# The place of one load of x among the set-up transfers of SyncE's queue in a fused two-block transformer kernel

## What is computed

```
m = silu(cond) @ w_ada + b_ada                     # nine rows: shift, scale, gate x 3
x = x + gate * self_attn(ln(x) * (1+scale) + shift)       # A: windows of 128 rows, 16 heads
x = x + gate * topk_cross_attn(ln(x) * (1+scale) + shift, ctx)   # B: best 16 of 77 keys
x = x + gate * swiglu(ln(x) * (1+scale) + shift)          # C: 256 -> 2 x 1024 -> 256
kv = modulated layernorm(ctx)                       # the second context
x = x + cross_attn(modulated layernorm(x), kv) @ Wp + bp  # D: softmax over 77 keys
```

## Time and profile before

| | |
|---|---|
| median of 3 runs | 1042.06 us (1039.88 to 1044.54) |
| the profiled execution's own time | 1043.68 us |
| its span, first to last instruction | 1041.9 us |
| mean granted TensorE clock | 0.971 of full |
| TensorE busy (matmul) | 983.6 us, 94% |
| VectorE, ScalarE, GpSimd busy | 834.8, 782.9, 705.4 us |
| load of x, two per tile | 64 transfers in all, median 2.2 us to landing |
| store of y, two per tile | 64 transfers in all, median 2.1 us |

### The profile page before, as it was taken

The page is one execution under the profiler, slowest core; times in us unless marked ns, Lnnn a source line. Parts: engine busy times, 40 slices in busy tenths (PEclk is TensorE's granted clock), DMA queues, the critical chain, the costliest instruction groups (busy, mean ns, idle before and its releaser), DMA issues.

```text
span 1041.9 us, 33051 instructions
## 1 busy us (share of the span) xinstructions
PE 983.6 (94%) x10980; PEld 868.1 (83%) x10980; DVE 834.8 (80%) x4234; ACT 782.9 (75%) x1681; POOL 705.4 (68%) x1100
## 2 busy tenths in 40 slices
PE   6885699999999999999999999999999999999985
PEld 5563588898888898889988888988999888888874
DVE  2356789989888888889898888888898988888631
ACT  1143478888888888888888888888888888888662
POOL 2257355777777778777777777787777777767754
PEclk9788699999999999999999999999999999999996
DMA  8305000000000000000000000000000000000000
GB/s 294 42 27 125 32 7 8 7 12 13 13 13 11 4 12 12 13 13 12 12 12 12 13 10 4 13 12 12 13 13 12 12 12 8 7 8 7 7 6 16
DMA packets 33848, 23.14 MB, mean 22 GB/s; under 512 B 22979, under 2 KB 31427, under 8 KB 33168
## 3 DMA queue, kind: packets, MB, share of 16 engines
q1 hardware_dynamic: 33680, 21.02, 7.8%
HBM read 16.19 MB, written 4.83 MB: 20 GB/s over the span
## 4 chain that ended last, share of the span: by engine, by line
PE 87%; issue 3%; DMA 3%; DVE 3%; SPq 2%; ACT 2%; POOL 2%; POOLq 0%; DVEq 0%; ACTq 0%
PE ps L1242 21%; PE ps L1251 10%; PE ps L1123 9%; PE ps L1231 8%; PE ps L1220 7%; PE ps L1204 7%; PE ps L1195 4%; PE ps L1154 3%; PE ps L1171 3%; PE ps L1184 3%; PE ps L1112 2%; PE ps L1134 2%; PE ps L1144 2%; DMA w_mod_sb<-in_w_mod 1%; PE ps L1053 1%
## 5 line engine op out<-in xcount | busy, mean ns | idle before, releaser
L1242 PE MATMUL ps<-hT_C,w_m_sb 128*128 128x128 f32 x2048 | 250.7, 275 | 0.2 <-DVE hidden_C L934 0.2
L1242 PEld LDWEIGHTS ps<-hT_C,w_m_sb 128*128 128x128 f32 x2048 | 241.6, 192 | 2.7 <-issue 0.7
L678 ACT ACTIVATE silu_C<-ps,cols_sb 128x128 f32<-128x128 f32 x256 | 90.7, 367 | 72.9 <-PE ps L1242 72.0
L503 POOL TENSOR_TENSOR p_D<-scores_D,rc_D 128x616 f32<-128x616 f32 x64 | 78.2, 1225 | 79.1 <-DVE rc_D L905 79.1
L503 POOL TENSOR_TENSOR p_B<-p_B,rc_B 128x616 f32<-128x616 f32 x64 | 77.8, 1217 | 67.4 <-DVE p_B L891 66.1
L1251 PE MATMUL ps<-w_m_sb,hidden_C 128*128 128x256 f32 x512 | 121.0, 379 | 0.0
L934 DVE SCALAR_TENSOR_TENSOR hidden_C<-ps,cols_sb,silu_C 128x128 f32<-128x128 f32 x256 | 87.9, 344 | 33.4 <-ACT silu_C L678 33.0
L883 DVE MATCH_REPLACE8 scores_left_B<-mx_B,scores_left_B 128x77 f32<-128x77 f32 x512 | 108.3, 223 | 0.0
L879 DVE MATCH_REPLACE8 scores_left_B<-mx_B,scores_B 128x77 f32<-128x77 f32 x512 | 108.1, 222 | 0.2 <-issue 0.2
L1251 PEld LDWEIGHTS ps<-w_m_sb,hidden_C 128*128 128x128 f32 x512 | 94.6, 190 | 11.4
L833 DVE TENSOR_REDUCE mx_A<-ps 128x8 f32<-128x1024 f32 x64 | 75.4, 1221 | 26.8 <-PE ps L1154 26.6
(11 more groups left out here) (180 smaller groups left out, 2574.6 us busy)
## 6 DMA issues: line engine op xcount, KB each, us to landing
x_A<-in_x SPq DMA_DIRECT2D x64, 64.0 KB, 2.2
out<-y_D SPq DMA_DIRECT2D x64, 64.0 KB, 2.1
w_mod_sb<-in_w_mod SPq DMA_DIRECT2D x2, 1024.0 KB, 11.9
w_m_sb<-in_w_m SPq DMA_DIRECT2D x1, 2048.0 KB, 7.6
w_m_sb<-in_w_m SPq DMA_DIRECT2D x1, 1024.0 KB, 10.0
w_qkv_sb<-in_w_qkv SPq DMA_DIRECT2D x1, 768.0 KB, 5.8
w_gate_sb<-in_w_gate SPq DMA_DIRECT2D x1, 768.0 KB, 7.5
rows_sb<-in_rows SPq DMA_DIRECT2D x1, 768.0 KB, 8.8
```

Of the source, the lines that this page charges most:

```text
L503: g.tensor_tensor(where, src, rc, ALU.mult).then_inc(n_ok[s], 1)
L678: sc.activation(SA[:, j, :], bank(f"C.up{j}")[:, 0:P], ACT.Silu, bias=col("bm1_a", j)).then_inc(sa_ok, 1)
L1242: ins = mm(bank(f"C.up{j}")[:, half * P:(half + 1) * P], w_m1[:, k, m:m + P], HT["C"][:, t % HT_COPIES["C"], k, :], start=(k == 0), stop=( ...
```

## The change

In SyncE's `body` the loading of the MLP weights moves from the head of body 4 to its end, and the rearrangement of the second context ("D") moves from the end of body 3 to the end of body 4, ahead of the MLP weights. So the load of x for tile 4 (the fifth), which stands in body 4, is now issued before both, and the two keep their order between themselves.

```diff
             def body(i):
-                if starts(i, 4):
-                    load_mlp_weights()
                 run(load_next_x, i, 0)
                 run(store_y, i, 9)
                 if starts(i, 2):
                     set_up_flat("B")
                     load_context_weights()
-                if starts(i, 3):
+                if starts(i, 4):
                     set_up_flat("D")
+                    load_mlp_weights()
```

## The result

The changed kernel takes 1032.91 us (median of 5 runs, 1028.8 to 1034.12) against 1042.06 (median of 5); the ratio is 0.9909, with a 95% interval of 0.9891 to 0.9928. Repeated in two further sessions it gave 0.9921 (0.9899 to 0.9943) and 0.9931 (0.9911 to 0.9952). So it is 0.7 to 0.9% faster, 7.2 to 9.4 us by the medians, clear of the 0.5% that can be told from nothing. Its profiled execution has a span of 1032.3 us and a time of 1034.12; the span before was 1041.9.

What follows compares the result with a forecast made beforehand. TensorE bounds the long middle; before it, VectorE stalls 10.94 us for x behind 3 MB in the same queue. A gain of 8.9 - 0.4 = 8.5 us on the median of 1042.06 gives 1033.5 us, range 1029 to 1038.

Steps and rivals of the forecast that it cites:

- (a): SyncE's load of x for tile 4: issued at about 66.4 us, so VectorE's stall of 10.94 us goes wholly.
- (b): SyncE's rearrangement and MLP weights, now behind the load's wait: start as before, cost nothing, at most 1 us.
- (c): TensorE after VectorE's statistics of tile 4: restarts at 97.97 us, 10.9 us earlier.
- (d): ScalarE's copies wait for GpSimd's clearing until 103.1 us; 2.0 of 10.9 us are spent there, L1184 moves by 8.9.
- (e): From L1184 on everything moves by 8.9 us, carried to the end; VectorE waits about 4 us before ev_A.
- (f): GpSimd's vblk_D beside a working VectorE: stays at 4.95 us, with an upper bound of about 6.9.
- rival of a slow vblk_D: GpSimd's vblk_D becomes slow beside VectorE: gain 6.9 us, 1035.2 us; chance 0.08.
- (g): TensorE's clock at L1184 after idle time: half clock costs nothing or about 0.9 us; 0.4 taken.
- a rival with a chance of 0.15: TensorE's half-clock stretch at 125 to 131 us need not recur: gain 11 to 13.5 us, 1028.6 to 1031; chance 0.15.
- rival of the instructions caught in the flood of transfers: Engines' instruction fetches held up by full DMA engines at 98 to 107 us: gain 1.7 to 6 us; chance 0.08.

Runs made afterwards that it cites:

- held: The changed kernel, with the fifth load of x also waiting for the normalisation of tile 3: 1043.32 us, ratio 1.0021 to the kernel before.
- no_pad_wait: The changed kernel without ScalarE's wait for GpSimd's clearing: 1030.90 us, ratio 0.9891 to the kernel before; in another session (_b) 1030.50 us.
- mlp_first: The changed kernel with the MLP weights issued ahead of the rearrangement, behind x: 1034.22 us, ratio 0.9924 to the kernel before.
- x_between: The kernel before, with the fifth load of x issued between the two MLP weights: 1038.73 us against 1041.65, ratio 0.998.
- x_behind_flat: The kernel before, with the fifth load of x ahead of the MLP weights but still behind the rearrangement: 1032.24 us, ratio 0.9907.

## Why the prediction was right

The forecast was 1033.5 us, a gain of 8.5; measured are 1032.91 and 9.2 in the first session. By its steps:

- (a) held: xn_A was the last to come, x was issued at 65.40 (66.4 said), and st_A stands without a wait at 96.05 (96.3).
- (b) held, and the run *held* gives its price: once the wait ends after the values are ready, each us costs one.
- (c) held: TensorE restarts at 97.74 (97.97).
- (d) was the step that mattered, and held: the clearing ends at 103.52 (103.06), the copies start at 103.60, and no_pad_wait shows that it is this wait. It is 0.5 us later than I had it, since the whole rearrangement is 0.7 later in this execution. What it costs was mis-sized: I had 2.0 us. Removing it brought 2.9 and 3.7. With L1204 at half clock, as I had reckoned, L1184 starts 19.6 us after the start of the rearrangement (no_pad_wait) instead of 22.0 (the changed kernel's first trace), 2.4 us earlier, and its 32 matmuls run at full clock, 1.08 us instead of 2.15 (106.90 to 109.05): the wait costs by the clock too, and I had kept the two apart. With L1204 at full clock L1184 starts 17.3 us after it (no_pad_wait_b), but then GpSimd's queue is the limit: o_A is 3.1 us earlier than in the changed kernel of that session.
- (e) held in its second half: the TensorE-bound middle carries the shift to the end, as the last column shows. Its first half, that from L1184 on everything moves alike, did not: the first matmul of the MLP moved 9.85 us where ev_A moved 7.4 (see g). And VectorE waits 5.69 us before ev_A, not about 4, for ev_A comes 1.5 us later than I had it.
- (f) held: vblk_D takes 4.95 us beside a working VectorE, to the digit the value of before, and its instructions 1271 to 1275 ns each. The rival of a slow vblk_D fell. The two slow ones of vblk_B lie beside w_out_B again. With the rule that I had set beside it (the Trainium skill, SBUF — State Buffer, "Who interferes with whom") the trace agrees for w_out_B (2261 ns for the slowest of vblk_B beside it). MATCH_REPLACE and MAX8 ran beside all of vblk_D and cost it nothing. I had MATCH_REPLACE read two tiles; in the timeline it is two instructions, MATCH_VALUE_LOAD and MATCH_REPLACE8, so it is no test of a rule on two inputs of one instruction. The price of that rival, 6.9 us, left the 0.4 us of (g) out; by my own sum it would have been 6.5, and 1035.5.
- (g) is the term that was mis-sized, in both its halves. L1219 and L1183 both ran at half clock, so that the 32 matmuls of L1183 took 2.15 us instead of 1.08: 1.1 us, where I had taken 0.4 of a possible 0.9. They also started 0.4 us later than I had them (106.90, for 106.5), from the later clearing of (d). So ev_A moved by 7.4 us, not 8.9 or 8.5. Against that, the low stretch behind ev_A was missing: 2.5 us, which I had put into a rival with a chance of 0.15. That the sum came out this close was luck: these errors cancelled. The other traces of the changed kernel have the low stretch partly (1.61 us for L1153) and nearly wholly (2.04), and the two further sessions gave 9.4 and 7.2 us.

The rival of the instructions caught in the flood of transfers fell with the changed kernel itself: TensorE restarts at 97.74 us and L1183 at 106.90, and the DMA share of that kernel's window 97 to 107 us is 0.93. Without the wait for the clearing all engines run through the flood, at a DMA share of 0.84 (columns as in the earlier trace rows):

```profile
96.00:107.00 11.00, 7.76 (x115) 6.32 (x115) 9.34 (x67) 6.09 (x11) 10.38 (x15) 0.84 0.84 305
```

It also fell with mlp_first, where the flood lies at 66 to 78 us beside four engines that work (TensorE is busy 7.81 of these 12 us, VectorE 11.24). The queues of that window of its trace:

```profile
q1 hardware_dynamic: 448, 3.28, 73.4%
q8 instruction: 1, 0.02, 0.6%
q14 instruction: 2, 0.02, 0.3%
```

Three packets of instructions pass in it, and no engine shows a wait that they would explain. That agrees with the Trainium skill (DMA: Bandwidth & Descriptors, "Queues, rings and completion order"), by which a DMA engine takes turns between its queues. The run *x_between* shows that within one queue x does wait its turn.

## What to carry to other kernels

A small load that the pipeline needs soon should not stand behind a bulk load that is needed late: here 64 KB took 9.4 us behind 3 MB, and moving it ahead cost nothing, while the bulk had some 16 us to spare. Before moving it, look at what its own wait will hold up in the same queue, as that costs one for one (held). And when a stall of 11 us is removed, look for the next release that used to be hidden in it; here it was a semaphore that covered more than the step needed, worth another 3 us. The gap in the profile did not name it: "issue" stood where a semaphore was waited for.

## What the runs showed beside that

- TensorE's clock differs between executions of one kernel at the same place. After a wait of 1.1 us, L1203 of the changed kernel took 1.29 us in one trace, 2.37 and 2.19 in the others. A sum made from one trace can be wrong by 1 to 2 us for this alone.
- The profile's "issue" before ScalarE's copy was a wait for a semaphore that GpSimd's clearing raises; it showed no releaser in any of the seven traces in which TensorE had been done well before. In x_behind_flat, where the clearing and the transposes ended within 0.1 us of each other, it named TensorE.
- The rearrangement starts between 81.3 and 84.9 us in the thirteen traces other than held's, although nothing ahead of it differs but the place of x and of the weights. That scatter of 3.6 us goes into the times as it is, and is as large as the effects of the smaller experiments, so the stretches of the table tell more than the times of single executions.
- One float32 matmul of the program is two in the trace (28 came out as 56), which I had overlooked in sizing the added work.
